# A gated graph network in fp32: the n gate's product on the edge sums is added onto r*hn in PSUM, by TensorE

## The reference, cut to what matters

```python
for l in range(4):
    m = h @ weight[l]
    agg = segment_sum(m[src], dst)           # over the edges
    gi = agg @ w_ih.T + b_ih                 # three gates r, z, n
    gh = h @ w_hh.T + b_hh
    r = sigmoid(i_r + h_r)
    z = sigmoid(i_z + h_z)
    n = tanh(i_n + r * h_n)                  # the change is about this line
    h = (1 - z) * n + z * h
x = layernorm(x + (h + x))
```

## Time and profile before

| what | value |
|---|---|
| median of 3 runs | 2330.45 us (2329.63 to 2331.1) |
| span of the profiled execution | 2327.4 us |
| the runs' median above that span | 3.05 us |
| TensorE busy in the span | 2229.5 us (96%) |
| VectorE busy | 2175.6 us (93%) |
| ScalarE busy | 1842.3 us (79%) |
| GpSimd busy | 1719.4 us (74%) |
| mean granted TensorE clock | 0.986 |

### The profile page before, as it was taken

The page is one execution under the profiler, slowest core; times in us unless marked ns, Lnnn a source line. Parts: engine busy times, 40 slices in busy tenths (PEclk is TensorE's granted clock), DMA queues, the critical chain, the costliest instruction groups (busy, mean ns, idle before and its releaser), DMA issues.

```text
span 2327.4 us, 49180 instructions
## 1 busy us (share of the span) xinstructions
PE 2229.5 (96%) x11728; PEld 1898.3 (82%) x11728; DVE 2175.6 (93%) x4211; ACT 1842.3 (79%) x3483; POOL 1719.4 (74%) x1654
## 2 busy tenths in 40 slices
PE   3999999999999999999999999999989999999996
PEld 2888888888878888888878888888877888888885
DVE  7899999999879999999969999999969999999998
ACT  1688888888768888888857888888856888888886
POOL 3877777777487777777558777777748888888884
PEclk7999999999999999999999999999999999999998
DMA  2455555555545555555545555555544555555554
GB/s 58 120 155 160 158 160 161 158 160 160 157 131 173 171 173 172 174 172 173 166 127 172 172 171 172 173 174 171 174 130 122 159 156 155 155 155 154 155 155 118
DMA packets 277064, 362.45 MB, mean 156 GB/s; under 512 B 107754, under 2 KB 186586, under 8 KB 276980
## 3 DMA queue, kind: packets, MB, share of 16 engines
q1 hardware_dynamic: 238118, 309.12, 43.5%
q0 software_dynamic: 38784, 52.30, 9.7%
q10 hardware_dynamic: 78, 0.08, 0.0%
HBM read 208.71 MB, written 179.20 MB: 167 GB/s over the span
## 4 chain that ended last, share of the span: by engine, by line
PE 66%; DVE 18%; issue 10%; ACT 2%; DMA 2%; POOL 1%; DVEq 1%; SPq 0%; ACTq 0%; POOLq 0%
PE pZ L847 17%; PE pR L847 8%; PE pHN L847 8%; PE pA L835 8%; PE pO L929 5%; PE pIN L847 4%; PE pA L847 4%; DVE bn L1442 3%; PE pR L891 3%; PE pR L888 3%; PE pR L889 3%; DVE diff L1411 3%; DVE aggT L1381 3%; DVE y_rows L1435 2%; PE pH L786 2%
## 5 line engine op out<-in xcount | busy, mean ns | idle before, releaser
L683 POOL DMA_INDIRECT gath<-state,idx x900 | 931.4, 1035 | 264.6 <-issue 255.8
L660 POOL TENSOR_TENSOR h_lo<-hT,h_hi 128x500 fp32r<-128x500 f32 (+1 forms) x400 | 375.8, 940 | 200.5 <-ACT h_hi L1050 149.7
L683 POOL DMA_INDIRECT gath<-in_x_dram,idx x300 | 321.9, 1073 | 101.8 <-issue 68.7
L1080 ACT ACTIVATE rg<-pR,bsum 128x500 f32<-128x500 f32 x400 | 269.7, 674 | 112.2 <-PE pR L891 100.2
L1400 DVE SCALAR_TENSOR_TENSOR narg<-pHN,bhh,rg 128x500 f32<-128x500 f32 x400 | 292.3, 731 | 44.9 <-ACT rg L1080 44.1
L1372 DVE TENSOR_TENSOR a_lo<-aggT,a_hi 128x500 fp32r<-128x500 f32 x396 | 271.5, 686 | 0.3
L1062 ACT CAST sel<-sel 128x504 fp32r (+1 forms) x400 | 245.9, 615 | 31.6 <-DVE flag_i L1356 29.5
L1417 DVE TENSOR_TENSOR diff<-pZ,diff 128x500 f32<-128x500 f32 x400 | 267.7, 669 | 0.8
L1381 DVE TENSOR_TENSOR aggT<-pA,hT 128x500 f32<-128x500 f32 x396 | 263.8, 666 | 1.7 <-PE pA L835 1.6
L1088 ACT ACTIVATE pZ<-pZ,bsum 128x500 f32<-128x500 f32 x400 | 256.1, 640 | 0.0
L1067 ACT CAST a_hi<-aggT 128x500 fp32r<-128x500 f32 x396 | 235.6, 595 | 6.5 <-DVE aggT L1381 6.5
(11 more groups left out here) (211 smaller groups left out, 6384.1 us busy)
## 6 DMA issues: line engine op xcount, KB each, us to landing
columns<-newT SPq DMA_DIRECT2D x300, 250.0 KB, 2.3
hT<-columns SPq DMA_DIRECT2D x300, 250.0 KB, 2.7
state<-o_rows SPq DMA_DIRECT2D x300, 224.0 KB
x_rows<-in_x_dram SPq DMA_DIRECT2D x200, 224.0 KB
out_dram<-o_rows SPq DMA_DIRECT2D x91, 224.0 KB
gath<-state,idx POOLq DMA_INDIRECT x900, 2.4
state<-o_rows SPq DMA_DIRECT2D x297, 26.0 KB
idx<-edge_src SPq DMA_DIRECT2D x395, 1.5 KB
```

The costliest lines, as they stand in the source:

```text
L660: nc.gpsimd.tensor_tensor(part_of(h_lo, u)[:, cols], hT[:, u % RING, cols], part_of(h_hi, u)[:, cols].bitcast(F32), ALU.subtract).then_inc ...
L683: pool.indirect_dma_start(out=gath[:, u % RING, j, :], out_offset=None, in_=states[l], in_offset=bass.IndirectOffsetOnAxis(ap=idx[:, u % R ...
L1080: nc.scalar.activation(rg[:, :], pR[:, 0:COLS], ACT.Sigmoid, bias=bsum[:, 0:1]).then_inc(s_r, 1)
```

## The change

For all blocks but the first four of a layer (`seeded`), VectorE writes r*hn into the n gate's PSUM bank instead of into `narg`, and TensorE adds the three matmuls of the product on the sums onto it (`n_onto_r_times_hn`, start=False), at the end of the step, after the z product and before the transposes. The add on VectorE is gone. ScalarE applies tanh in place in that bank, as the first instruction of the next step. VectorE makes difference and product of block b-1 at the start of step b, directly ahead of the new state of b-1, and then r*hn of b. On ScalarE, the high part of the state comes ahead of the r gate, and so does the first half of `normalise`, but in every fifth block. In layer 3 GpSimd makes 350 columns of `h_lo` instead of 500, VectorE the other 150. The order of the first four steps stays but for the place of the r gate.

```diff
+LOW_BY_POOL = COLS, COLS // 2, COLS // 2, 350
+ADDED_APART = RAMP
+        def seeded(i, u):
+            return not (isinstance(i, int) and i == 0 and u < ADDED_APART)
@@ TensorE
+            def n_onto_r_times_hn(l, b, u):
+                pe.wait_ge(s_t1, l * NB + b + 1)
+                product(l, u, n_bank(u), 2, ("in",), False, True, True).then_inc(s_IN, 1)
-                        n_on_sums(l, b, u, l * NB + b - 1 if l or exists_before(i, u, 2) else None)
+                        if not onto:
+                            n_on_sums(l, b, u, l * NB + b - 1 if l or exists_before(i, u, 2) else None)
...
+                        if onto:
+                            n_onto_r_times_hn(l, b, u)
                         if not first:
                             pb, pu, _ = after(i, u, -1)
                             turn_back(l, pb, pu, isinstance(i, int) and pb == 0,
@@ ScalarE
+            def n_gate_in_place(l, b, u):
+                act.wait_ge(s_IN, l * NB + b + 1)
+                nc.scalar.activation(n_bank(u), n_bank(u), ACT.Tanh, bias=bih[:, 2:3]).then_inc(s_n, 1)
...
+                        if exists_before(i, u, ADDED_APART + 1):
+                            n_gate_in_place(l, *after(i, u, -1)[:2])
                         if not ramp:
                             rows(i, u)
+                            high()
+                        fresh = half_done(i, u, OUTLAG) if final else None
+                        if not fresh:
+                            normal(i, u, 0)
                         r_gate(l, b, u, first and l == 0)
+                        if fresh:
+                            normal(i, u, 0)
...
-                        n_gate(l, b, u)
+                        if not seeded(i, u):
+                            n_gate(u, l * ADDED_APART + b + 1)
@@ VectorE
+            def r_times_hn_below_in(l, b, u):
+                g = l * NB + b
+                dve.wait_ge(s_HN, g + 1)
+                dve.wait_ge(s_r, g + 1)
+                v.scalar_tensor_tensor(n_bank(u), pHN[:, 0:COLS], bhh[:, 2:3], rg[:, :],
+                                       ALU.add, ALU.mult).then_inc(s_t1, 1)
...
-                        if last:
-                            renew(*after(i, u, -1))
-                        if ramp and u:
+                        if exists_before(i, u, ADDED_APART + 1):
+                            difference(l, *after(i, u, -1)[:2])
+                            product(l, *after(i, u, -1)[:2])
+                        if onto or u:
                             renew(*after(i, u, -1))
                         if ramp and u == 3:
                             aggregate(l, 4, 4)
-                        r_times_hn(l, b, u)
+                        if onto:
+                            r_times_hn_below_in(l, b, u)
+                        else:
+                            r_times_hn(l, b, u)
+                            n_argument(l, b, u)
                         if shifted:
                             shift(*shifted)
-                        if not ramp and not last:
-                            renew(*after(i, u, -1))
-                        n_argument(l, b, u)
...
-                        difference(l, b, u)
+                        if not onto:
+                            difference(l, b, u)
...
-                        product(l, b, u)
+                        if not onto:
+                            product(l, b, u)
```

More of the change, by code:

```diff
@@ L30 @@
 CAP = TILES * P
-HALF = COLS // 2
+LOW_BY_POOL = COLS, COLS // 2, COLS // 2, 350
 RING = 5
@@ L381, in on_from, with shared @@
             return None
-        def halved(l):
-            return 0 < l < L - 1
+        def shared(l):
+            return LOW_BY_POOL[l] < COLS
+        def seeded(i, u):
+            return not (isinstance(i, int) and i == 0 and u < ADDED_APART)
         def unsplit(l, b):
@@ L654, in split_h @@
             def split_h(l, b, u, behind=None, whole=False, ready=1):
-                cols = slice(0, COLS if whole or not halved(l) else HALF)
+                cols = slice(0, COLS if whole else LOW_BY_POOL[l])
                 pool.wait_ge(s_hhi, l * NB + b + ready)
@@ L836, in sum_edges, with product @@
                 last.then_inc(s_pA, 1)
-            def product(l, u, bank, c, sides, begins=True, ends=True):
+            def product(l, u, bank, c, sides, begins=True, ends=True, onto=False):
                 passes = []
@@ L847, in product @@
                     last = nc.tensor.matmul(bank, w, xx, start=begins and k == 0,
-                                            stop=ends and k == len(passes) - 1)
+                                            stop=ends and k == len(passes) - 1, skip_group_check=onto)
                 return last
@@ L938, in step @@
                         ramp = isinstance(i, int) and i == 0 and u < RAMP
-                        r_on_state(l, b, u, start, halved(l))
+                        onto = seeded(i, u)
+                        r_on_state(l, b, u, start, shared(l))
                         if not start:
@@ L1080, in r_gate, with n_gate @@
                 nc.scalar.activation(rg[:, :], pR[:, 0:COLS], ACT.Sigmoid, bias=bsum[:, 0:1]).then_inc(s_r, 1)
-            def n_gate(l, b, u):
-                act.wait_ge(s_t2, l * NB + b + 1)
+            def n_gate(u, added):
+                act.wait_ge(s_t2, added)
                 nc.scalar.activation(n_bank(u), narg[:, :], ACT.Tanh, bias=bih[:, 2:3]).then_inc(s_n, 1)
+            def n_gate_in_place(l, b, u):
+                act.wait_ge(s_IN, l * NB + b + 1)
+                nc.scalar.activation(n_bank(u), n_bank(u), ACT.Tanh, bias=bih[:, 2:3]).then_inc(s_n, 1)
             def z_gate(l, b, u):
@@ L1151, in step, with high @@
                         ramp = isinstance(i, int) and i == 0 and u < RAMP
+                        coming = on_from(l, i, u, PRE)
+                        def high():
+                            if coming:
+                                nl, nb, nu, ni = coming
+                                high_h(nl, nb, nu, TURNS * (nl - 1) + turn(ni, nu) + 1)
+                        if exists_before(i, u, ADDED_APART + 1):
+                            n_gate_in_place(l, *after(i, u, -1)[:2])
                         if not ramp:
                             rows(i, u)
+                            high()
+                        fresh = half_done(i, u, OUTLAG) if final else None
+                        if not fresh:
+                            normal(i, u, 0)
                         r_gate(l, b, u, first and l == 0)
+                        if fresh:
+                            normal(i, u, 0)
                         if ramp:
@@ L1158, in step @@
                             rows(i, u)
[L1159 to L1167, removed]
+                            high()
+                        if coming and coming[0] == l and not ramp and not final:
+                            if not opening(i):
+                                high_gathered(l, *coming[1:3], turn(*coming[:1:-1]))
+                            widen(l, *coming[1:3])
                         if ramp and u == 1:
@@ L1171, in step @@
                             widen(l, 4, 4)
-                        normal(i, u, 0)
                         if final and not ramp and exists(i, u, 3):
                             widen(l, *after(i, u, 3)[:2])
-                        n_gate(l, b, u)
+                        if not seeded(i, u):
+                            n_gate(u, l * ADDED_APART + b + 1)
                         if ramp and u < 3:
@@ L1189, in fast_path @@
                     blocks(act, step)
+                    n_gate_in_place(l, NB - 1, UNROLL - 1)
                     for k in range(lag, 0, -1):
@@ L1205, in one @@
                         r_gate(l, b, 0, first and l == 0)
-                        n_gate(l, b, 0)
+                        n_gate(0, l * NB + b + 1)
                         z_gate(l, b, 0)
@@ L1364, in low_h @@
                 dve.wait_ge(s_hhi, l * NB + b + 1)
-                v.tensor_tensor(part_of(h_lo, u)[:, HALF:COLS], hT[:, u % RING, HALF:COLS],
-                                part_of(h_hi, u)[:, HALF:COLS].bitcast(F32), ALU.subtract).then_inc(s_hlov, 1)
+                cols = slice(LOW_BY_POOL[l], COLS)
+                v.tensor_tensor(part_of(h_lo, u)[:, cols], hT[:, u % RING, cols],
+                                part_of(h_hi, u)[:, cols].bitcast(F32), ALU.subtract).then_inc(s_hlov, 1)
             def low_part(l, b, u, summed=False):
@@ L1532, in step @@
                         coming = on_from(l, i, u, PRE)
-                        coming = coming if coming and halved(coming[0]) else None
+                        coming = coming if coming and shared(coming[0]) else None
                         if coming and not ramp and not last:
```

## The result

The changed kernel takes 2388.11 us (median of 4 runs, 2386.77 to 2391.76) against 2330.77 (4 runs, 2329.63 to 2331.84) for the kernel before: a ratio of 1.0246 [1.0232, 1.0261], 57.3 us slower. The forecast was 2388. The profiled execution took 2388.16 us, with a span of 2386.2.

The account below looks back on a forecast made before the run. TensorE was taken to bound layers 0 to 2, VectorE layer 3. Terms 0 + 12.5 + 43.7 + 1.3 = 57.5 us, added to the 2327.4 us span and 3.05 us, gave 2388 us; range 2346 to 2430.

Parts of the forecast that it names:

- What bounds before: Before the change, TensorE sets the pace in layers 0 to 2 (5.61, 5.21 us a block), VectorE in layer 3 (5.78).
- The loop, layers 1 and 2: Circle through r*hn, aggT, a_hi, z gate, tanh, difference, product, new state: 5.28 us a block against 5.21, 12.5 us lost.
- Layer 0: In layer 0 a block has 5.61 us, so the 5.28 us loop fits: nothing lost or gained.
- Layer 3: Loop plus half of normalise, 6.05 us; shift +0.83, moments 0.2 per five blocks; average 6.26 against 5.78, 43.7 us lost.
- End: At the very end, tanh of block 99 stands behind the z gate and half of normalise: 1.3 us.
- The covered wait on TensorE: TensorE's n product waits for r*hn, there after 2.16 us; TensorE arrives after 2.28, so covered by 0.12 us.
- that rival: TensorE stalls too: r*hn over 0.12 us late in layers 0 to 2, 29 us on top, 2417 us; chance 0.08.
- The clock: Full clock assumed despite TensorE idling 0.8 us a block in layer 3; rival: it falls, far above range, chance 0.02.
- What would show it: Layer 1: r gates 5.28 us apart, TensorE short of 200 us; layer 3: 6.05 apart, VectorE about 90%, tanh behind normalise.
- Only layer 3 gets longer: Rival: some link 0.07 us shorter, TensorE still paces layers 1 and 2; +45 us, 2375 us; chance 0.20.
- Faster by VectorE's relief: Rival: loop doesn't bind layer 3, which runs at VectorE's remaining 5.44 us a block; -31 us, 2299 us; chance 0.12.
- Dependent instructions cost no more: Rival: dependent VectorE instructions spaced like independent ones; layer 3 at 5.86 us, +7 us, 2339 us; chance 0.04.

Follow-up runs that it names:

- the fastest kernel: Last kernel measured: changed kernel with tanh ahead of a_hi, a_lo and h_lo in VectorE's gaps, both halves of normalise moved; 2312.66 us, ratio 0.9923.
- The copy inside and beside: Changed kernel plus an unused 500-column ScalarE copy in layers 1 and 2, between z gate and tanh (2481.01 us) or behind the r gate (2390.08 us).
- tanh first: Changed kernel with tanh in its own step ahead of a_hi of b+2, and a_lo between difference and product on VectorE; 2348.47 us, ratio 1.0081.
- only ScalarE's half: Changed kernel with tanh in its own step ahead of a_hi of b+2, a_lo left at its old place on VectorE; 2467.79 us, ratio 1.0582.
- the first of the two kernels with everything together: Changed kernel with tanh ahead of a_hi, a_lo and h_lo in VectorE's gaps, second half of normalise behind next r gate; 2319.63 us, ratio 0.9951.

## Why the prediction was right

- **What bounds before.** TensorE in layers 0 to 2, VectorE in layer 3: held. Even in the fastest kernel the relief of VectorE moved layer 1 only from 5.21 to 5.19 us; in layer 3 it paid, once the loop was shortened.
- **The loop, layers 1 and 2.** Links as forecast and as measured (0.65, 0.71 / 0.70, 0.50 / 0.52, 0.57, 0.68 / 0.67, 0.76 / 0.78, 0.82 / 0.81, 0.59): 5.28 and 5.29. The window averages 5.27. The copy inside and beside shows that this order is what costs.
- **Layer 0.** Costed at nothing; the window gives 0.02 us a block. Layers 0 to 2 together: 12.5 forecast, 13.3 measured with the new order in them alone.
- **Layer 3.** Normal block 6.05 against 6.03; shift +0.83 against +0.80; the moments' block takes +0.36 (r*hn at 1943.68 and 1950.07, 6.39 apart) where I took 0.2. Average 6.26 both times, since these small errors cancel; 43.7 for the blocks and 1.3 for the end were forecast, 45.0, and 43.4 measured with the new order in that layer alone.
- **End.** Tanh of the last block comes 1.33 us behind its z gate, as forecast; what of it reached the end of the span wasn't measured apart.
- **The covered wait on TensorE.** This step was wrong. The last r matmul starts at 1002.61 us, r*hn ends at 1004.78, 2.17 us later (2.16 forecast), and the first n matmul starts at 1004.87, 2.26 us later (2.28 forecast). But I left out the matmul's weight load, which in the trace starts some 0.23 us ahead of a matmul. That load waits 0.23 us in each block of layer 1. The wait is the circle's, not one of its own: r*hn stands behind the new state, 0.26 us after the end of the r gate, and with tanh first the same product runs at 5.19 us. The 29 us of that rival didn't come on top.
- **The clock.** 1.00 from 1900 to 2100 us with TensorE idle for 16 us in 200. One reading was wrong: the fall behind 3.5 us of idle time isn't the only one at a layer's end in the trace of before. At the end of layer 1 the clock fell to 0.50 too, behind 3.19 us without a matmul (1171.22 to 1174.41).
- **What would show it.** R gates 5.28 apart, tanh directly behind the second half, VectorE at 90% (180.64 of 200): seen. "TensorE short of 200 us in 200" was wrong as a sign; the busy time stayed at 200.00 and only counts and weight loads told.
- **Luck.** 57.5 forecast and 57.3 measured is closer than the method is. Layer 3 was 1.6 us too dear and layers 0 to 2 0.8 too cheap, and the four runs of the changed kernel alone spread over 5 us. The mechanism held; the last digits are luck.

**The rivals.** "Only layer 3 gets longer" falls by the run on layers 0 to 2 (+13.3 us, its interval above 1.003). "Faster by VectorE's relief" was the mechanism with a real gain behind it, but it needs a shorter loop; with the order shortened by hand layer 3 went from 6.26 to 5.54. "Dependent instructions cost no more" falls by the timeline of layer 1: 0.78 and 0.81 between instructions that depend on each other, 0.59 from the new state to r*hn, which doesn't; in the last kernel, with other work between, each spacing is 0.58 or 0.59 (0.22 behind the 150-column piece). The Trainium skill (VectorE: DVE Perf Modes, "The DRAIN you can't avoid") has a semaphore between two VectorE instructions at no extra cost. By that rule the forecast would have been 2339 us, and 2388 were measured; the trace doesn't agree.

**What stays open.** The few microseconds by which the `h_lo` split may matter, and the rest of the misses: about 6 us in the run with only ScalarE's half, and some 6 us in the first of the two kernels with everything together.

## What to carry to other kernels

When an edit takes work off one engine, follow the data and the order of every queue once round: if the path passes through each block once, add up the starts from one instruction to the next, and compare the sum with the block's length in every stage. Where the order written in the code closes such a circle, an instruction cost nothing measurable beside it, and inside it the whole step from its start to the next. Most of what I missed in size in the experiments was a stage or a block of five that I hadn't put through this sum; and the cure was to reorder, with independent work between dependent instructions.

## What the runs showed of the hardware

- R*hn written to PSUM takes 743 ns on average, against 731 into SBUF in the kernel before (735 for the 16 that the changed kernel still writes there), and its successor starts 0.65 us behind it in both. Tanh in place takes 639 ns instead of 682 with its input in SBUF. Groups of equal shape, changed kernel:

```profile
L1438 DVE SCALAR_TENSOR_TENSOR pA<-pHN,bhh,rg 128x500 f32<-128x500 f32 x192 | 142.7, 743 | 13.1 <-ACT rg L1094 13.1
L1102 ACT ACTIVATE pA<-pA,bih 128x500 f32<-128x500 f32 x192 | 122.6, 639 | 1.8 <-PE pA L852 1.8
```

- Dependent VectorE instructions of 128x500, directly behind one another, start 0.78 to 0.81 us apart; with independent work between, difference and product are followed after 0.58 or 0.59 (the last kernel, layer 3).
- TensorE can show 200.00 of 200 us busy and do 1% less; the count of matmuls (1075 to 1063) and the weight loads' busy time (173.25 to 167.25) show it.
